# Four residual layers on one core: earlier staging of the last weights, an earlier first tile, and a convolution kernel made head by head

## The reference, cut to what matters

```python
# layer 0: a state-space convolution per head, masked by length
K = 2.0 * einsum('hn,hnl->hl', Cs, exp(dtA[:, :, None] * arange(L))).real      # N = 64 modes per head
x = x + mask * (causal_conv(x * mask, K) + x * mask * D[:, None])
# layer 1: x W1' and a top-2 mixture of 8 rank-16 adapters; layer 2: x W2' and one of 5 rank-32 adapters
# layer 3: x W3q', W3q = W3 plus low rank, quantised group by group to a codebook
x = x + L1(x); x = x + L2(x); x = x + L3(x)
```

## Time and profile before

| | us |
|---|---|
| three runs, median (lowest, highest) | 995.47 (992.75, 996.88) |
| the profiled execution, its own time | 991.54 |
| its span, first to last instruction | 989.7 |
| around the span (the difference) | 1.8 |
| PE busy | 974.8 |
| DVE busy | 842.5 |
| ACT busy | 456.2 |
| POOL busy | 281.1 |

### The profile page before, as it was taken

One profiled execution on the slowest core, in us unless ns is written; L12 is line 12 of the kernel. 1 busy time (PEld: TensorE's weight loads), 2 busy tenths in 40 slices (PEclk: granted clock), 3 DMA queues, 4 the chain that ended last, 5 costly groups with the idle time before them and its releaser, 6 DMA issues.

```text
span 989.7 us, 16510 instructions
## 1 busy us (share of the span) xinstructions
PE 974.8 (98%) x4705; PEld 786.5 (79%) x4705; DVE 842.5 (85%) x1651; ACT 456.2 (46%) x862; POOL 281.1 (28%) x346
## 2 busy tenths in 40 slices
PE   9999999999999999999999999999999999999997
PEld 5465559877878788888888888888888888888886
DVE  6799999999955789888988888888888888889863
ACT  3342426252755554454544554445545445454531
POOL 6510000766344323222233222332222322223200
PEclk9999999999999999999999999999999999999999
DMA  8814010101113356645455455565555655556421
GB/s 292 128 27 86 0 43 1 43 1 19 25 22 67 60 91 117 104 90 106 91 110 107 92 104 95 105 112 93 99 98 97 117 98 97 99 96 116 80 43 43
DMA packets 370485, 82.05 MB, mean 83 GB/s; under 512 B 343170, under 2 KB 363586, under 8 KB 370450
## 3 DMA queue, kind: packets, MB, share of 16 engines
q1 hardware_dynamic: 369442, 80.90, 43.1%
q10 hardware_dynamic: 1008, 0.76, 0.3%
HBM read 60.88 MB, written 20.71 MB: 82 GB/s over the span
## 4 chain that ended last, share of the span: by engine, by line
PE 76%; ACT 1%; issue 1%; DVE 1%; DVEq 0%; ACTq 0%
PE bank L789 35%; PE bank L1024 10%; PE bank L776 7%; PE bank L755 5%; PE bank L810 5%; PE bank L766 4%; PE bank L744 4%; PE bank L780 4%; PE bank L816 1%; PE bank L800 1%; PE bank L805 0%; PE bank L794 0%; PE bank L986 0%; PE bank L1013 0%; PE bank L975 0%
## 5 line engine op out<-in xcount | busy, mean ns | idle before, releaser
L789 PE MATMUL bank<-Mh,strips_r 128*128 128x512 f32 x1020 | 289.1, 395 | 0.0
L789 PEld LDWEIGHTS bank<-Mh,strips_r 128*128 128x128 f32 x1020 | 189.9, 188 | 40.9
L1101 ACT ACTIVATE SK<-ZZ 64x448 f32<-64x448 f32 x128 | 73.9, 577 | 214.2 <-DVE ZZ L1458 211.9
L550 POOL TENSOR_TENSOR Cl<-QC,Ch 128x256 fp32r<-128x256 f32 x32 | 39.1, 1223 | 449.7 <-ACT Ch L1083 449.7
L789 PE MATMUL bank<-Ml,strips_r 128*128 128x512 f32 x510 | 159.9, 395 | 0.0
L1458 DVE SCALAR_TENSOR_TENSOR ZZ<-ZZ,coef 128x192 f32<-128x192 f32 (+1 forms) x256 | 106.9, 457 | 10.1 <-DVE ZZ L1449 0.3
L789 PEld LDWEIGHTS bank<-Ml,strips_r 128*128 128x128 f32 x510 | 95.9, 188 | 22.6
L956 PE MATMUL bank<-E,A 128*128 128x512 f32 (+1 forms) x320 | 97.8, 466 | 0.0
L1449 DVE SCALAR_TENSOR_TENSOR ZZ<-ZZ,coef 128x384 f32<-128x384 f32 (+1 forms) x128 | 79.9, 624 | 13.5 <-DVE ZZ L1458 6.7
L956 PEld LDWEIGHTS bank<-E,A 128*128 128x128 f32 x320 | 51.0, 191 | 44.9 <-issue 44.4
L776 PE MATMUL bank<-Ml,strips_r 128*128 128x296 f32 x256 | 70.7, 299 | 0.0
(11 more groups left out here) (319 smaller groups left out, 1863.1 us busy)
## 6 DMA issues: line engine op xcount, KB each, us to landing
X<-in_x SPq DMA_DIRECT2D x256, 64.0 KB, 2.6
XT<-in_x SPq DMA_DIRECT2D x256, 64.0 KB, 2.5
out_x<-O SPq DMA_DIRECT2D x62, 256.0 KB, 3.3
toep<-kpad SPq DMA_DIRECT2D x128, 64.0 KB, 2.2
E<-in_L_cond_W SPq DMA_DIRECT2D x8, 512.0 KB, 9.3
vq<-in_L_cond_weight SPq DMA_DIRECT2D x8, 512.0 KB, 3.7
turned<-TB SPq DMA_DIRECT2D x29, 128.0 KB, 2.3
Bt<-turned SPq DMA_DIRECT2D x116, 32.0 KB, 2.2
```

What stands on the lines that cost most here:

```text
L789: pe.matmul(psO[nh][:, :], xs[:, c, :], ms[:, c, nh * BANK:(nh + 1) * BANK], start=(c == 0 and n == 0), stop=False)
L1101: act.activation(SK[ri * N:(ri + 1) * N, hh, :].rearrange("p (c b) -> p c b", b=B), ZZ[hh * N:(hh + 1) * N, :, ri, :], ACT.Copy).then_inc( ...
```

## The change

- The four staging jobs of the next quarter stand after mt = 2, 4, 6 and 7.
- In the last quarter state columns, first QB, first transposed states, first chunk states and Vt (in two parts) come one tile of `order` sooner. DVE makes X1T and X2T ahead of its first `turn_q`.
- The kernel is made in one piece ahead of m(3, 4): for each of the 64 heads one matmul with a stationary X1T of 4 columns and a moving Vt of 32 columns. Head a of each group of four writes PSUM partitions 32a to 32a+3, a column group of its own. D is added by DVE in PSUM, ACT makes Kh and DVE Kl in four pieces of 4 partitions x 512, and each piece is stored by a DMA of its own. Kt, its copies and its transposes are gone. DVE waits for the kernel ahead of the first two carry levels; Kl stands between the second and the third.

```diff
-                if q + 1 < QUARTERS and mt in (3, 5, 7, 8):
-                    order += [("a3", q + 1, (3, 5, 7, 8).index(mt))]
+                if q + 1 < QUARTERS and mt in (2, 4, 6, 7):
+                    order += [("a3", q + 1, (2, 4, 6, 7).index(mt))]
-        KERN_IN = 5
+        KERN_IN = 4
# SP
-                sp.dma_start(Drow[:, :], D_skip.rearrange("(a h) -> a h", a=1)).then_inc(ld_d, 16)
+                for a in range(PARTS):
+                    sp.dma_start(Drow[a * SPAN:a * SPAN + 1, :], D_skip.rearrange("(a h) -> a h", a=1)).then_inc(ld_d, 16)
...
-                    sp.wait_ge(ready, 1)
-                    sp.dma_start(bass.AP(kpad.tensor, part * KP + P, [[2 * KP, H], [1, P]]), t[:, :].bitcast(F32)).then_inc(kpad_stored, 16)
+                    for a in range(PARTS):
+                        sp.wait_ge(ready, a + 1)
+                        sp.dma_start(bass.AP(kpad.tensor, 2 * KP * a + part * KP + P, [[SPAN, PARTS], [2 * KP * PARTS, H // PARTS], [1, SPAN]]),
+                                     t[a * SPAN:a * SPAN + PARTS, :].rearrange("p (g r) -> p g r", r=SPAN).bitcast(F32)).then_inc(kpad_stored, 16)
# PE
-                def kern(part):
-                    if part == 0:
-                        pe.wait_ge(cols_ready, 2)
...
-                    for g in range(part * H // 16, (part + 1) * H // 16):
-                        heads = slice(4 * g, 4 * g + 4)
-                        last = pe.matmul(bank[2][:, 16 * g:16 * (g + 1)].rearrange("p (h k) -> p h k", k=PARTS),
-                                         Vt[:, heads, :].rearrange("p h r -> p (h r)"), X1T[:, heads, 0:PARTS], start=True, stop=True)
+                def kern():
+                    pe.wait_ge(cols_ready, 3)
+                    pe.wait_ge(tab_out, 1)
+                    pe.wait_ge(m_taken, M_LAST)
+                    for g in range(H // PARTS):
+                        for a in range(PARTS):
+                            last = pe.matmul(bank[2][a * SPAN:a * SPAN + PARTS, g * SPAN:(g + 1) * SPAN], X1T[:, PARTS * g + a, 0:PARTS],
+                                             Vt[:, PARTS * g + a, :], start=True, stop=True)
+                    last.then_inc(kern_full, 1)
-                def kern_transpose():
...
-                        if (q, mt) == (LAST_Q, KERN_IN) and kt < 4:
-                            kern(kt)
+                        if (q, mt, kt) == (LAST_Q, KERN_IN, 0):
+                            kern()
...
-                    if j == ("m", LAST_Q, 3):
+                    if j == ("m", LAST_Q, 2):
                         state_transpose(0, first=True)
-                    elif j == ("m", LAST_Q, 4):
+                    elif j == ("m", LAST_Q, 3):
                         for hh in range(HB):
                             chunk_states(0, hh, first=True)
                     elif j == ("m", LAST_Q, 5):
-                        kern_transpose()
                         state_transpose(1)
# ACT: state_columns after m(3, 0); x_hi(0) and the first half of Vt after (3, 1); b_hi(0) and the second half
# after (3, 2); states_in(0) after (3, 3); then
                         elif j == ("m", LAST_Q, 4):
-                            states_in(0, first=True)
-                            act.wait_ge(kern_full, 1)
-                            for a in range(4):
...
+                            act.wait_ge(kf_ready, PARTS)
+                            for a in range(PARTS):
+                                rows = slice(a * SPAN, a * SPAN + PARTS)
+                                act.activation(Kh[rows, :], bank[2][rows, :], ACT.Copy).then_inc(kh_ready, 1)
# DVE
+                dve.wait_ge(kern_full, 1)
+                dve.wait_ge(ld_d, 16 * PARTS)
+                for a in range(PARTS):
+                    first = bank[2][a * SPAN:a * SPAN + 1, ::SPAN]
+                    dve.scalar_tensor_tensor(first, first, 1.0, Drow[a * SPAN:a * SPAN + 1, a::PARTS], ALU.add, ALU.add).then_inc(kf_ready, 1)
                 dve.wait_ge(cols_ready, 1)
                 for level in range(2):
                     carry(0, level)
                     carry_across(0, level)
...
+                for a in range(PARTS):
+                    rows = slice(a * SPAN, a * SPAN + PARTS)
+                    dve.wait_ge(kh_ready, a + 1)
+                    dve.tensor_tensor(Kl[rows, :], bank[2][rows, :], Kh[rows, :].bitcast(F32), ALU.subtract).then_inc(kl_ready, 1)
                 for level in range(2, len(LEVELS)):
```

More of the change, by code:

```diff
@@ L125, in resid_stack_kernel @@
     mrow = place("mrow", [P, MULT], F32)
-    Drow = place("Drow", [1, H], F32)
+    Drow = place("Drow", [P, H], F32)
     half_pi = place("half_pi", [P, 1], F32)
@@ L164, in resid_stack_kernel @@
     assert cursor[0] <= region_q + 4 * (5 * QCOLS + 2 * 1024)
-    Kh = place("Kh", [H, P], F32R)
-    Kl = place("Kl", [H, P], F32R)
     assert cursor[0] <= region_q + 4 * (5 * QCOLS + 2 * 1024)
@@ L172, in resid_stack_kernel @@
     Bt = place("Bt", [P, HB, P], F32)
+    Kh = place("Kh", [P, H // PARTS * SPAN], F32R)
+    Kl = place("Kl", [P, H // PARTS * SPAN], F32R)
     assert cursor[0] <= at_expo
@@ L219, in resid_stack_kernel @@
     Cl = place("Cl", [P, HB, P], F32R)
-    Kt = place("Kt", [SPAN, PARTS, H], F32)
     assert cursor[0] <= at_quant3 + 4 * QCOLS
@@ L261, in resid_stack_kernel @@
         exp_ready, exp_done, cols_ready, a3_pad = sem("exp_ready"), sem("exp_done"), sem("cols_ready"), sem("a3_pad")
-        kern_full, kern_taken, kernT_full = sem("kern_full"), sem("kern_taken"), sem("kernT_full")
+        kern_full = sem("kern_full")
         kf_ready, kh_ready, kl_ready = sem("kf_ready"), sem("kh_ready"), sem("kl_ready")
@@ L484, in _ @@
                 for part, t, ready in ((0, Kh, kh_ready), (1, Kl, kl_ready)):
-                    sp.wait_ge(ready, 1)
-                    sp.dma_start(bass.AP(kpad.tensor, part * KP + P, [[2 * KP, H], [1, P]]), t[:, :].bitcast(F32)).then_inc(kpad_stored, 16)
-                sp.wait_ge(kpad_stored, 48)
+                    for a in range(PARTS):
+                        sp.wait_ge(ready, a + 1)
+                        sp.dma_start(bass.AP(kpad.tensor, 2 * KP * a + part * KP + P, [[SPAN, PARTS], [2 * KP * PARTS, H // PARTS], [1, SPAN]]),
+                                     t[a * SPAN:a * SPAN + PARTS, :].rearrange("p (g r) -> p g r", r=SPAN).bitcast(F32)).then_inc(kpad_stored, 16)
+                sp.wait_ge(kpad_stored, 16 + 32 * PARTS)
                 load_toep(0)
@@ L697, in _ @@
                             pool.wait_ge(m_lo, n + 1)
-                        if j == ("m", LAST_Q, 1):
+                        if j == ("m", LAST_Q, 0):
                             pool.wait_ge(cols_ready, 1)
@@ L976, in a3 @@
                         ps[:, m * P:(m + 1) * P], qq[q][:, m % QT_TILES, (2 * n + m // QT_TILES) * P:(2 * n + m // QT_TILES + 1) * P], ident[:, :]))
-                def kern(part):
-                    if part == 0:
-                        pe.wait_ge(cols_ready, 2)
-                        pe.wait_ge(tab_out, 1)
-                        pe.wait_ge(m_taken, M_LAST)
-                    for g in range(part * H // 16, (part + 1) * H // 16):
-                        heads = slice(4 * g, 4 * g + 4)
-                        last = pe.matmul(bank[2][:, 16 * g:16 * (g + 1)].rearrange("p (h k) -> p h k", k=PARTS),
-                                         Vt[:, heads, :].rearrange("p h r -> p (h r)"), X1T[:, heads, 0:PARTS], start=True, stop=True)
-                    if part == 3:
-                        last.then_inc(kern_full, 1)
-                def kern_transpose():
[L992 to L995, removed]
+                def kern():
[7 more added lines that the diff above has]
+                    last.then_inc(kern_full, 1)
                 def m(q, mt):
@@ L1198, in state_columns, with kernel_rows @@
                     last.then_inc(cols_ready, 1)
-                def kernel_rows():
-                    act.activation(Vt[lo_n, :, :], pow_r[lo_n, :, 0:SPAN], ACT.Copy)
-                    act.activation(Vt[hi_n, :, :], pow_i[hi_n, :, 0:SPAN], ACT.Copy).then_inc(cols_ready, 1)
+                def kernel_rows(part):
+                    rows, power = ((lo_n, pow_r), (hi_n, pow_i))[part]
+                    act.activation(Vt[rows, :, :], power[rows, :, 0:SPAN], ACT.Copy).then_inc(cols_ready, 1)
                 lo_n, hi_n = slice(0, N), slice(N, 2 * N)
@@ L1348, in _ @@
                             sines(1)
+                        elif j == ("m", LAST_Q, 0):
+                            state_columns()
                         elif j == ("m", LAST_Q, 1):
-                            state_columns()
-                        elif j == ("m", LAST_Q, 2):
                             for hh in range(HB):
                                 x_hi(0, hh, first=True)
-                            kernel_rows()
+                            kernel_rows(0)
+                        elif j == ("m", LAST_Q, 2):
+                            b_hi(0, first=True)
```

(23 more changed lines are left out.)

3 lines of the change are left out of this document (removed).

## The result

The changed kernel takes **987.94 us** (median of 4, 986.36 to 988.15) against 994.55 (4 runs, 992.75 to 996.88): a ratio of 0.9926, 95% interval 0.9906 to 0.9945, 0.74% faster. The forecast was 993.3, the range 989.0 to 998.5: the direction was right, the size not, and the time lies outside the range. The profiled execution took 988.15 us, its span is 986.3. Against the profiled execution of before that is only -3.4 us, while the medians differ by 6.6. So nearly half of the gain is not in this pair of profiles and needs an explanation of its own.

The account below looks back on a forecast made before the run. PE's time was taken to bound the kernel; stagings -3.6, old kernel gone -3.7, new kernel +5.0 and a new wait +0.2 summed to -2.1 us on the 995.47 median: 993.3 us, range 989 to 998.5.

Parts of the forecast that it names:

- What bounds it: Whole kernel: PE, busy 974.8 of 989.7 us, sets the time; only PE time counts and the loop moves as a block.
- Part 1: Quarter ends: stagings one tile sooner close two holes (3.20 us) and give 0.39 at the first end, 3.6 us saved.
- Part 2: Old convolution kernel: its four parts, transposes and three switches go from PE, saving 3.7 us.
- part 4: Last quarter: QB transposes after m(3, 5) newly wait 0.2 us for POOL; other waits stay covered.
- Part 3: New convolution kernel ahead of m(3, 4): 128 records at 39 ns each, adding 5.0 us.
- the lowest bound: New convolution kernel: four column groups at work together, limited by the stream, need 0.9 us.
- fast kernel: Rival, new convolution kernel: groups overlap, 7 to 25 ns a record, 0.9 to 3.2 us; 989.2 to 991.5; chance 0.18.
- the thinnest cover: Last quarter's chunk states: DVE's low parts of x and B ready 0.7 us before PE wants them.
- The clock: Rival: clock falls to 1.2 GHz behind the 128 records, m(3, 4) takes 3.46 us more, 996.8; chance 0.05.
- The base of my sum: Time of the kernel before, to which the summed difference was applied: median 995.47 us; profiled execution 991.54.

Follow-up runs that it names:

- group by group: Changed kernel with the convolution kernel's 64 matmuls reordered, all 16 of one column group before the next, instead of four groups by turns: 988.79 us, ratio 0.9944.

## Why the prediction was wrong, and where it was right

- **What bounds it**: right. PE's time ahead of the loop is what moved. From the loop's start to the end every trace but one shows 664.8 to 665.5 us, and the first tile keeps its wait (1.3 us in every trace); the one with 666.6 had a fall of the clock behind it.
- **Part 1, the stagings, 3.6 us**: by the two executions without a fall 2.1. The second end gave its 1.4. The first gave nothing instead of 0.4: ACT, behind its comparisons, had Bw_parts 0.8 us later and not 0.47, which used up the hole behind it, and the wait grew to 2.40. The third gave 0.6 of 1.8: I had BW and the last two tiles cover the ACT copy and "most of any diagonals", without a price for the diagonals at this end. They took 0.86 us before; sooner, they run beside DVE's tables and take 3.49 us, behind two low parts.
- **Part 2, what goes, 3.7 us**: right, 3.9 by the starts of the traces. From m(3, 0) to the loop the whole was measured at -2.58: -3.9 for the old kernel, +1.18 for the new, +0.3 for a new wait (part 4), and -0.2 for a shorter way to and through the first chunk states.
- **Part 3, 39 ns a record**: the step that failed most. I had 0.9 us as the lowest bound and argued myself off it with L994, four records that all write the same partitions. The row that mattered was L1013, whose groups work at once. Measured: 9.2 ns by turns, 27.3 group by group. The rival "fast kernel" (0.18) was the case for the kernel, near its low end, and puts the time at 989.5. The Trainium skill's floor of about 25 ns between two matmuls (TensorE: Matmul & The Clock Gate, Back-to-back issue gap) is above the 9.2 ns measured here, and its 62 ns in software are out; its warning against tiling an already small dimension (TensorEngine Tiling (Array Packing), Instruction Overhead) did not hold for this size, where the tiled kernel took 1.18 us and the old one with its transposes 3.44. The measurements decide.
- **Part 4**: right. The wait of the QB transposes was there: they start at 304.01, 7.2 us behind the kernel's end where two tiles take 6.9, so 0.3 us for 0.2. No wait at the chunk states, at the kernel or at L755. DVE's low parts took 1.29 us for 2.32, so that what I called the thinnest cover, 0.7 us, was about 1.6.
- **The clock**, a term that I put at nothing for the kernel before. I took it as a rival for the changed kernel alone and gave it 0.05 since "No row shows a fall". One execution showed none; 13 of 25 others had a mean clock of 0.995 or less. What is taken away with the holes and the old kernel is not only their idle time, but 1.7 us behind a hole and up to 3.3 in the old kernel, in part of the runs. Without any fall the change is worth 4.7 us by the starts of the loop, and 5.4 by the lowest runs (991.81 against 986.42); the loop's own 664.8 to 665.5 us can hold most of that difference. The medians' 6.6 hold the falls as well, which before had more often. The base of my sum, one execution and a median 3.9 us apart, was the hint that I passed over.
- **The sum put right**: -2.1 - 3.7 + 1.2 + 0.3 = -4.3, 991.2 on my base. Two errors were in part each other's remedy: part 1 promised 1.5 us too much, part 3 charged 3.8 too much. With all four parts right the forecast would still have been 3.2 us too high: 0.9 because the base itself, 995.47, became 994.55 with a fourth run, and the rest by the clock and by what the loop differs between executions, which these runs don't separate further.

## What to carry to other kernels

When a kernel's runs spread by more than the profiled one explains, look at the clock of several executions in stretches of a few microseconds around each PE wait: closing a hole of 1 to 2 us can return up to 1.7 us more in the runs in which the clock fell behind it, and make all runs alike. One profile without a fall says little: of two profiles of the changed kernel one had it behind the first hole, the other in tile 0. Small matmuls are nearly free if neighbours use different column groups and there are few enough of them in a row. Work moved sooner meets other neighbours: price it beside what runs then, above all POOL beside DVE.

## What the runs showed of the hardware that I had not expected

- 128 float32 records of 4 stationary and 32 moving columns in 1.18 us, 9.2 ns each, over four column groups; 27.3 ns in one group.
- 512 such records in a row: PE stops for 2.24, 2.45 and 1.57 us, after 210, 128 and 128 of them, with no wait in the profile. 128 in a row bring no stop.
- A PE wait of 2.4 us is followed by the lower clock in some executions and not in others of the same kernel, at 1.7 us each; one of 1.3 us likewise, at 1.9.
- 3.49 us of small matmuls in one column group at a time, with PE busy throughout, were not followed by the lower clock in the one execution traced; within 3.6 us of the old kernel's in one piece it fell, in the one traced.
- Two POOL additions of 128x128: 0.86 us alone, 3.49 us beside a busy DVE.
